# A curvature flow stage on four engines: one numerator moved to GpSimd, three results moved to PSUM, the border copy moved to VectorE, and new instruction orders

## The reference

```
def step(u):
    ux, uy   = conv(u, SOBEL_X), conv(u, SOBEL_Y)          # 3 x 3, per channel
    uxx, uxy, uyy = conv(ux, SOBEL_X), conv(ux, SOBEL_Y), conv(uy, SOBEL_Y)
    each of the five is clipped to -10 .. 10
    g2 = ux*ux + uy*uy
    K = clip((uxx*uyy - uxy*uxy) / ((1 + g2)**2 + EPS), -5, 5)
    H = clip(((1 + uy*uy)*uxx - 2*ux*uy*uxy + (1 + ux*ux)*uyy) / (2*sqrt(1 + g2 + EPS)**3 + EPS), -5, 5)
    u = u + 0.01 * clip(alpha*K + beta*H, -1, 1)
    return the inner 30 x 30 of u, with the border filled from its neighbours
u = step applied 10 times; result = 0.7*u + 0.3*x
```

## Time and profile before

| | us |
|---|---|
| three executions | 785.02, 787.89, 787.63 |
| the profiled execution | 785.12 |
| its span, first to last instruction | 783.3 |
| PE busy | 662.1 |
| DVE busy | 457.5 |
| ACT busy | 387.6 |
| POOL busy | 267.6 |

### The profile page before, as it was taken

How to read it: one execution, slowest core, us unless ns; L and a number is a source line. 1 busy time by engine, 2 the same in 40 slices (tenths; PEclk the granted TensorE clock), 3 DMA queues, 4 the chain that set the end, 5 groups by cost and what they waited for, 6 DMA issues and landing times.

```text
span 783.3 us, 11067 instructions
## 1 busy us (share of the span) xinstructions
PE 662.1 (85%) x4334; PEld 464.9 (59%) x4334; DVE 457.5 (58%) x682; ACT 387.6 (49%) x656; POOL 267.6 (34%) x235
## 2 busy tenths in 40 slices
PE   5897899999966666789988988989998998998992
PEld 4784684564422233444555767777777777777771
DVE  5630000293211012223434899999999999999996
ACT  1300000150000000112222799999999999999995
POOL 1000000000034200000002676777677677677662
PEclk9898799999985788999999999999999999999996
DMA  9989999999999999999950000000000000000001
GB/s 348 427 355 406 414 419 415 427 418 412 427 375 405 419 428 427 427 427 428 423 198 25 0 1 0 0 0 0 0 0 0 0 0 0 0 0 0 0 0 54
DMA packets 20946, 166.53 MB, mean 213 GB/s; under 512 B 1840, under 2 KB 2224, under 8 KB 11568
## 3 DMA queue, kind: packets, MB, share of 16 engines
q1 hardware_dynamic: 19552, 162.60, 50.4%
q0 software_dynamic: 688, 2.04, 0.8%
q10 hardware_dynamic: 672, 1.41, 0.5%
HBM read 164.99 MB, written 1.05 MB: 212 GB/s over the span
## 4 chain that ended last, share of the span: by engine, by line
ACT 30%; PE 29%; DMA 24%; DVE 11%; issue 6%; ACTq 0%; POOLq 0%; POOL 0%; DVEq 0%; SPq 0%
DMA ring<-wout_w 14%; PE bank L374 8%; PE bank L390 6%; ACT ring L1059 4%; PE bank L517 4%; ACT ring L1046 4%; PE bank L491 4%; PE bank L436 4%; ACT bank L1035 3%; ACT ring L1042 3%; DMA ring<-wv_w 3%; DMA ring<-wqk_p 3%; DMA ring<-wout_p 3%; ACT ring L1041 2%; ACT ring L1034 2%
## 5 line engine op out<-in xcount | busy, mean ns | idle before, releaser
L568 PE MATMUL bank<-u_parts,vmr 128*128 128x480 f32 x1360 | 305.5, 382 | 33.9 <-DVE ring L854 33.2
L568 PEld LDWEIGHTS bank<-u_parts,vmr 128*128 128x128 f32 x1360 | 252.5, 188 | 87.0 <-DVE ring L854 48.5
L390 PE MATMUL bank<-ring,small 128*32 128x256 f32 x1152 | 81.9, 434 | 33.0 <-DMA ring<-wout_w 29.0
L1137 POOL TENSOR_TENSOR ring<-ring 128x480 f32<-128x480 f32 x40 | 49.2, 1230 | 95.9 <-DVE reg_a L884 74.2
L390 PEld LDWEIGHTS bank<-ring,small 128*32 128x32 f32 x1152 | 40.1, 122 | 67.4 <-issue 26.5
L390 PE MATMUL bank<-ring,xw 128*32 128x256 f32 x1024 | 64.1, 410 | 15.6 <-DMA ring<-wv_w 15.6
L374 PE MATMUL bank<-reg_a,ring 128*128 128x256 f32 x256 | 61.7, 406 | 6.2 <-ACT reg_a L939 3.4
L695 DVE SCALAR_TENSOR_TENSOR reg_a<-bank,prm 128x512 f32<-128x512 f32 x4 | 2.8, 691 | 103.2 <-PE bank L443 103.2
L374 PEld LDWEIGHTS bank<-reg_a,ring 128*128 128x128 f32 x256 | 52.2, 206 | 15.2 <-DMA ring<-wqk_p 3.7
L390 PEld LDWEIGHTS bank<-ring,xw 128*32 128x32 f32 x1024 | 34.0, 117 | 43.9 <-DMA ring<-wv_w 19.2
L990 ACT ACTIVATE reg_e<-xa 32x384 f32<-32x384 f32 (+7 forms) x20 | 9.1, 457 | 96.5 <-DVE xa L824 70.2
(11 more groups left out here) (193 smaller groups left out, 982.7 us busy)
## 6 DMA issues: line engine op xcount, KB each, us to landing
ring<-wv_w SPq DMA_DIRECT2D x32, 2048.0 KB, 23.6
ring<-wout_w SPq DMA_DIRECT2D x30, 2048.0 KB, 36.8
ring<-wqk_p SPq DMA_DIRECT2D x4, 2048.0 KB, 19.8
ring<-wqk_w SPq DMA_DIRECT2D x4, 2048.0 KB, 20.2
ring<-wv_p SPq DMA_DIRECT2D x2, 2048.0 KB, 19.9
ring<-wout_p SPq DMA_DIRECT2D x2, 2048.0 KB, 22.8
ring<-wout_w SPq DMA_DIRECT2D x4, 1024.0 KB, 36.1
vmr<-vmats POOLq DMA_DIRECT2D x1, 1664.0 KB, 7.2
```

The lines of the kernel that those rows point to most:

```text
L390: ins = te.matmul(bank[32 * j:32 * j + 32, b_, n0:n0 + 256], lhs(c), slot[k % NSLOT][:, c, 256 * j:256 * j + 256], start=start and c == 0, ...
L568: last = te.matmul(dst[:, 0:NF], mat(m, first), p3[:, 2 + off:S + off, :], start=(high and n == 0), stop=(not high and n == len(terms) - 1))
L1137: p.tensor_tensor(abs_[n], ab[n][:, 0:NF], ab[n][:, NF:2 * NF], ALU.add).then_inc(po["absum"], 1)
```

## The change

It touches the curvature stage only. In words:
- The numerator of K, uxx*uyy minus the squared mixed field, is formed by GpSimd in slot k instead of by VectorE in slot k+1. ScalarE writes the squared mixed field to a tile in SBUF (`sqm`), where GpSimd reads it, and leaves the field itself in PSUM.
- The Relu of the H end term is written by ScalarE into the mixed field's bank, and VectorE's difference and its clamp are formed there in place. The addition to u reads it from there.
- The clamp and the addition to u are done one slot later (`older`, slot k-2), at the head of VectorE's slot.
- The border copy goes from ScalarE to VectorE, to the end of its slot.
- TensorE makes the mixed field last instead of first, with a semaphore of its own (`fldxy`).
- ScalarE puts the mixed square ahead of the cross term, and the high part between the second logarithm and the last exponential. GpSimd forms the sum of the outer products in slot k and the low part one slot later, and no longer waits for u.
- VectorE runs one slot more at the end (SLOTS + 2), and the results of chunks 0 and 1 are written behind slot 41 instead of behind slot 40.

```
--- TensorE, fields()
-                    te.wait_ge(ve["num"], k - 2)
-                stencil(bank[:, b1 + 2, :], u_hi[c], first, UXY, True)
+                    te.wait_ge(ve["kh"], k - 2)
+                stencil(bank[:, b1, :], u_hi[c], first, UX, True)
                 te.wait_ge(po["lo"], k)
...
                 ins.then_inc(pe["fld2"], 1)
+                if reuse:
+                    te.wait_ge(ve["u"], k - 2)
+                stencil(bank[:, b1 + 2, :], u_hi[c], first, UXY, True)
+                stencil(bank[:, b1 + 2, :], u_lo[c], first, UXY, False).then_inc(pe["fldxy"], 1)
--- VectorE, slot_step(k, q, c, new, old, older), n = 1 - q, in its new order
+                mixed = lambda s_: fields_in(s_, 2)[:, 0, :]
+                if older:
+                    v.wait_ge(ve["diff"], k - 2)
+                    v.tensor_scalar(mixed(q), mixed(q), mid, DT, ALU.subtract, ALU.min).then_inc(ve["clipd"], 1)
                 if new:  clip of ux, uy        (waits fld1 k)
+                if older:
+                    v.wait_ge(ve["clipd"], k - 2)
+                    inner = u[c][:, 2 * B:S * B]
+                    v.scalar_tensor_tensor(inner, mixed(q), -DT, inner, ALU.max, ALU.add).then_inc(ve["u"], 1)
                 if old:  kh                    (waits num, hn, inv k-1)
                 if new:  clip of uyy, uxx      (waits fld2 k)
                          slope                 (waits sqr k)
                          clip of mixed         (waits fldxy k)
                          outer, cross          (cross waits cxy, sqxy k)
                 if old:
                     v.wait_ge(ac["ends"], k - 1)
+                    v.scalar_tensor_tensor(mixed(n), end_k[n], ten_ab[:, 0:1], mixed(n),
+                                           ALU.min, ALU.add).then_inc(ve["diff"], 1)
+                if older:
+                    v.wait_ge(ve["u"], k - 2)
+                    v.tensor_copy(u3(c)[:, 1:S + 1:S - 1, :], u3(c)[:, 2:S:S - 3, :]).then_inc(ve["pad"], 1)
--- ScalarE, slot_step(), in its new order
                 p2, sqr (k); up_h, end_k (k-1)
-                    a.activation(end_h[n], up_h[n], ACT.Relu, bias=ten_ab[:, 1:2],
+                    a.activation(fields_in(n, 2)[:, 0, :], up_h[n], ACT.Relu, bias=ten_ab[:, 1:2],
...
+                    a.wait_ge(ve["clipxy"], k)
+                    a.activation(sqm[q], fields_in(q, 2)[:, 0, :], ACT.Square).then_inc(ac["sqxy"], 1)
                     lnw, psq, w15, lnd (k)
+                    high(k + 2)                (waits ve["pad"] and pe["fldxy"] of k-2)
                     inv (k)
--- GpSimd, slot_step(), in its new order
                 hn (k-1)                       (waits absum, cross k-1)
                 cxy (k)                        (waits clip1 k)
+                low(k + 1)
                 m (k)                          (waits clip2 k)
+                    p.wait_ge(po["m"], k)
+                    p.wait_ge(ac["sqxy"], k)
+                    p.tensor_tensor(num[q][:, 0:NF], mxy[q], sqm[q], ALU.subtract).then_inc(po["num"], 1)
+                    p.wait_ge(ve["outer"], k)
+                    p.tensor_tensor(abs_[q], ab[q][:, 0:NF], ab[q][:, NF:2 * NF], ALU.add).then_inc(po["absum"], 1)
```

More of the change, by code:

```diff
@@ L578, in fields @@
                 if reuse:
[L579 to L580 removed]
+                    te.wait_ge(ve["kh"], k - 2)
+                stencil(bank[:, b1, :], u_hi[c], first, UX, True)
                 te.wait_ge(po["lo"], k)
[L582 to L588, removed]
+                stencil(bank[:, b1, :], u_lo[c], first, UX, False)
+                stencil(bank[:, b1 + 1, :], u_hi[c], first, UY, True)
+                stencil(bank[:, b1 + 1, :], u_lo[c], first, UY, False).then_inc(pe["fld1"], 1)
                 if reuse or c:
@@ L830, in f, with slot_step @@
                 return fld[par_][:, n * NF:(n + m) * NF]
-            def slot_step(k, q, c, new, old, first=False):
+            def slot_step(k, q, c, new, old, older, first=False):
                 n = 1 - q
[L835 to L838, removed]
+                mixed = lambda s_: fields_in(s_, 2)[:, 0, :]
+                two = lambda a_: a_.rearrange("p (x n) -> p x n", x=2)
+                if older:
+                    v.wait_ge(ve["diff"], k - 2)
+                    v.tensor_scalar(mixed(q), mixed(q), mid, DT, ALU.subtract, ALU.min).then_inc(ve["clipd"], 1)
@@ L849, in slot_step @@
+                if older:
+                    v.wait_ge(ve["clipd"], k - 2)
+                    if first and k - 2 <= NCH:
+                        v.wait_ge(ac["x3"], k - 2)
+                    inner = u[c][:, 2 * B:S * B]
+                    v.scalar_tensor_tensor(inner, mixed(q), -DT, inner, ALU.max, ALU.add).then_inc(ve["u"], 1)
                 if old:
-                    v.wait_ge(ve["num"], k - 1)
+                    v.wait_ge(po["num"], k - 1)
                     v.wait_ge(po["hn"], k - 1)
@@ L868, in slot_step @@
                     v.wait_ge(ve["clipxy"], k)
[L869 to L884, removed]
+                    v.wait_ge(ac["sqxy"], k)
+                    v.scalar_tensor_tensor(cxy[q], cxy[q], -2.0, mixed(q), ALU.mult, ALU.mult).then_inc(ve["cross"], 1)
+                if old:
+                    v.wait_ge(ac["ends"], k - 1)
+                    v.scalar_tensor_tensor(mixed(n), end_k[n], ten_ab[:, 0:1], mixed(n),
[3 more added lines that the diff above has]
+                    v.tensor_copy(u3(c)[:, 1:S + 1:S - 1, :], u3(c)[:, 2:S:S - 3, :]).then_inc(ve["pad"], 1)
             for n in ("alpha", "beta"):
@@ L914, in _ @@
             for k in range(1, LOOP_FROM):
-                slot_step(k, k % 2, (k - 2) % NCH, True, k > 1, True)
+                slot_step(k, k % 2, (k - 3) % NCH, True, k > 1, k > 2, True)
             with v.Fori(1, LOOPS + 1) as i:
                 for m in range(NCH):
[L918 to L921, removed]
+                    slot_step(i * NCH + (m + 3), (m + 3) % 2, m % NCH, True, True, True)
+            for k in range(LOOP_END, SLOTS + 3):
+                slot_step(k, k % 2, (k - 3) % NCH, k <= SLOTS, k <= SLOTS + 1, True)
+                for x in finished[k - SLOTS - 1] if k > SLOTS else ():
                     finish(x)
@@ L1045, in slot_step @@
                     a.wait_ge(ac["end_k"], k - 1)
-                    a.activation(end_h[n], up_h[n], ACT.Relu, bias=ten_ab[:, 1:2],
+                    a.activation(fields_in(n, 2)[:, 0, :], up_h[n], ACT.Relu, bias=ten_ab[:, 1:2],
                                  scale=neg_b).then_inc(ac["ends"], 1)
+                if new:
+                    a.wait_ge(ve["clipxy"], k)
+                    a.activation(sqm[q], fields_in(q, 2)[:, 0, :], ACT.Square).then_inc(ac["sqxy"], 1)
+                    a.wait_ge(ve["slope"], k)
+                    a.activation(lnw[q], slope[q], ACT.Ln, bias=D_EPS).then_inc(ac["lnw"], 1)
+                    a.activation(den[q][:, 0:NF], slope[q], ACT.Square).then_inc(ac["psq"], 1)
+                    a.wait_ge(ac["lnw"], k)
+                    a.activation(den[q][:, NF:2 * NF], lnw[q], ACT.Exp, bias=LN2, scale=1.5).then_inc(ac["w15"], 1)
+                    a.wait_ge(ac["psq"], k)
+                    a.wait_ge(ac["w15"], k)
+                    a.activation(den[q], den[q], ACT.Ln, bias=D_EPS).then_inc(ac["lnd"], 1)
+                if c is not None:
+                    high(k + 2, c, not first or k + 2 > NCH)
                 if not new:
                     return
[L1050 to L1059, removed]
                 a.wait_ge(ve["outer"], k)
@@ L1142, in slot_step @@
                     p.tensor_tensor(cxy[q], fld[q][:, 0:NF], fld[q][:, NF:2 * NF], ALU.mult).then_inc(po["cxy"], 1)
+                if c is not None:
+                    low(k + 1 if later else k + 2, c, later)
+                if new:
                     p.wait_ge(ve["clip2"], k)
                     p.tensor_tensor(mxy[q], fld[q][:, 3 * NF:4 * NF], fld[q][:, 4 * NF:5 * NF], ALU.mult).then_inc(po["m"], 1)
-                if c is not None:
-                    low(k + 2, c, later)
+                    p.wait_ge(po["m"], k)
[3 more added lines that the diff above has]
+                    p.tensor_tensor(abs_[q], ab[q][:, 0:NF], ab[q][:, NF:2 * NF], ALU.add).then_inc(po["absum"], 1)
             for x in range(2):
```

55 lines of the change are left out of this document (22 added, 33 removed).

## The result

| | us |
|---|---|
| four executions of the changed kernel | 800.71, 801.07, 799.89, 798.48 |
| their median; the median of four executions of the kernel before is 786.33 | 800.3 |
| ratio after / before, 95% interval | 1.0187 [1.0167, 1.0207] |
| the profiled execution and its span | 800.71, 798.6 |
| busy PE, DVE, ACT, POOL | 661.3, 470.5, 383.5, 317.9 |

What follows compares the result with a forecast made beforehand. VectorE and ScalarE, each waiting once per 8.50 us slot for the other, were taken to bound the kernel. Start -3.1, slots +6.3 and end +1.5 gave +4.7 on 787.63: 792.4 us, range 765 to 798.

Steps and rivals of the forecast that it cites:

- border copy held by the sum: VectorE's SBUF border copy waits 0.9 us for GpSimd's sum of outer products; slot 8.70 us, chance 0.62.
- 36 slots from the third kh to the 39th: Main run of the curvature loop, each slot taken at 8.70 us with the copy held: 313.2 us.
- the last slot: Final slot before kh(40), with no copy before it but GpSimd's hn: 7.84 us.
- what the end adds: Chunk 0 and 1 results behind the last difference, +1.33 us, and clamp and copies, +0.2: +1.5.
- first kh: VectorE's first kh instruction of the stage: at 438.1 against 441.20 before, a gain of 3.1 us.
- first to third kh: First two slots, at 8.70 us each less 0.2 because the first slot's copy finds GpSimd idle: 17.2 us.
- What holds the copy: At VectorE's slot end: a copy with both sides in SBUF waits until the running GpSimd instruction is through, 0.9 us.
- the second rival: Copy slips in front of GpSimd's sum, held by the numerator instead: slot about 8.05, 770 us, chance 0.05.
- the prediction's own signs: Copy record near 0.9 us ending with GpSimd's sum, slot 8.7, first kh near 438, ScalarE and TensorE idle over 0.6 per slot.
- The start: First mixed field at 432.9, then ScalarE's chain to the first kh at 438.1: -3.1 us from TensorE's order.
- The clamp in PSUM: VectorE's clamp of the difference, reading and writing PSUM: taken at 0.60 us, from 0.56 up to 0.63.
- The first rival: Border copy on VectorE not held by GpSimd: loop 8.02 us, time 769, bounds 765 and 775, chance 0.28.

Runs made afterwards that it cites:

- the early high part: Changed kernel with ScalarE making the high part for slots 3 and 4 right behind its squares in the first two slots: 790.84 us, ratio 1.0071.
- the copy from PSUM: Changed kernel with the border copy reading a PSUM bank instead of u in the 32 loop slots, border values not the reference's: 777.96 us, ratio 0.9903.
- the two and three repairs: Changed kernel with the early high part and VectorE's border formed from PSUM: 770.84 us; third, chunk 0 and 1 results written behind the last kh: 768.14 us.

## Why the prediction was wrong in size

By its own steps, from the profiled executions (spans 783.3 and 798.6, +15.3; forecast +4.7):

| step | forecast | measured |
|---|---|---|
| border copy held by the sum, slot | 8.70 | 8.72 |
| 36 slots from the third kh to the 39th | 313.2 | 314.0 |
| the last slot | 7.84 | 7.82 |
| what the end adds (last kh to the end of the span, 10.2 and 11.5) | +1.5 | +1.3 |
| first kh | 438.1 | 443.8, 442.8 without the later start |
| first to third kh | 17.2 | 21.5 |
| start of the stage | 0 | +1.0 |

- *What holds the copy* stood. Rows 5, one memset beside one VectorE instruction, carried the forecast of an instruction that the trace didn't have, and its place in the slot was right to 0.12 us: the sum starts at 610.12, the copy 0.21 behind it, 0.33 forecast. That place was close: 0.21 us earlier and the copy would have come ahead of the sum, which is the second rival at 770. Of the prediction's own signs the held copy, the slot and the idle time came as named (ScalarE and TensorE idle for 0.69 and 1.18 us per slot, from the busy table), and the first kh did not.
- *The start* is the step that failed: "432.9. From there to kh: 0.70 + 2.15 + 0.91 + 0.53 + 1.02 less 0.1 for the shorter first high part". That followed ScalarE's chain alone, and made the start a gain of 3.1 us. GpSimd's chain to the same kh has numerator, sum and hn behind a low part that in slots 1 and 2 waits for that very high part. I worked out GpSimd's order for the slots of the loop (`low(k + 1)`) and not for the written-out ones (`low(k + 2)`), where it differs. It cost 4.7 us in slot 1 and 4.3 in slot 2: 9.0, and the early high part gave 9.1 back (by the ratios). With the queue gone, the first kh stands 10.3 us behind the first clip, where the forecast has 10.5 (that clip comes eight matmuls of 0.224 sooner than the 429.35 of before, at 427.56, and 438.1 is 10.5 behind it), so the rest of that step holds. Without the 9.0 the span would have grown by 6.3, inside the range.
- *The clamp in PSUM* was taken at 0.60; its step is 0.62 to 0.63 (611.30 to 611.93), the upper bound, and over the 0.6 that the prediction gave as a sign that PSUM costs more. It isn't PSUM: the mixed clip in the same bank (L866, no per-partition scalar) keeps its step of 0.56 to 0.57. The slot came out 0.02 over the 8.70, which is the 0.8 us of the 36 slots.
- The start of the stage: its first matmul is at 425.07 before and 426.06 after. It differs from execution to execution (the first clip lies between 426.08 and 429.31 in the eight kernels here that have the new order), and the change doesn't touch what lies ahead of it. What moves it stays open; 1.0 of the 15.3 us is this.
- The first rival (not held: 8.02, 769) was well sized in its slot: 8.02, and the copy from PSUM shows 8.05. Its time of 769 was not reached by that alone (777.96), because the start that it counted as a gain was a loss; it is that of the two and three repairs, which mend the start as well.

## What to carry to other kernels

When an instruction moves to VectorE, look at where its operands lie and at what GpSimd does at that moment: with source and destination in SBUF, even a copy of 32 elements took until the GpSimd instruction beside it was through, and in every form run here an input in PSUM avoided it. An instruction with two SBUF inputs and its output in PSUM was not run. Read durations against the form's usual one, since busy shares and waits hide this. When orders change, follow each queue through the written-out first slots by themselves; what is in front of what may differ there from the loop, and here no later slot gave the loss back.

## What was not expected of the hardware

A hold can cost both engines in one slot: with GpSimd's wait gone from the kernel before, VectorE's difference went from 0.72 to 1.77 us, its clamp from 0.47 to 1.33, and GpSimd's hn from 1.23 to 1.53, and the slot from 8.50 to 10.39. Taking a wait away, with no work added, cost 8.9%.
